# Softmax in whole-tile operations and a pair of tiles half an iteration later, in a four-layer graph network

## What is computed

```python
def _gcn_layer(x, adj, W, b):                      # layer 2: three of them, relu after the first two
    return einsum('bnm,bmh->bnh', adj, x @ W) + b
x = layernorm(x + gcn3(x))
# layer 3: 8 heads of 64
q, k, v = x @ W_qkv
attn = softmax(where(mask, q @ k.T / 8, -big)) * 0.33
attn = attn + 0.33 * adj + 0.33 * exp(-adj)        # both masked
x = layernorm(x + (attn @ v) @ W_out + b_out)
```

## Time and profile before

| | us |
|---|---|
| median of three executions | 2944.71 |
| the profiled execution | 2944.47 |
| its span | 2942.7 |
| TensorE busy | 2735.9 (93% of the span) |
| VectorE busy | 1913.0 (65%) |
| ScalarE busy | 865.3 (29%) |
| GpSimd busy | 729.1 (25%) |

### The profile page before, as it was taken

One profiled execution on the slowest core, in us unless ns is written; L12 is line 12 of the kernel. 1 busy time (PEld: TensorE's weight loads), 2 busy tenths in 40 slices (PEclk: granted clock), 3 DMA queues, 4 the chain that ended last, 5 costly groups with the idle time before them and its releaser, 6 DMA issues.

```text
span 2942.7 us, 74056 instructions
## 1 busy us (share of the span) xinstructions
PE 2735.9 (93%) x30424; PEld 2283.0 (78%) x30424; DVE 1913.0 (65%) x4010; ACT 865.3 (29%) x2429; POOL 729.1 (25%) x1069
## 2 busy tenths in 40 slices
PE   6999999999999999579999999999999999999998
PEld 4778788778888778467877887887787788788777
DVE  5888888888888888545545545554554554554465
ACT  2222222222222222223323323332332332333233
POOL 1222222333333333122122213212211220321221
PEclk9999999999999999889999999999999999999999
DMA  5000000001000000111001001101100100110100
GB/s 172 27 30 30 30 31 32 31 30 30 31 30 31 30 31 30 50 50 36 12 26 37 27 11 37 32 10 33 37 19 19 37 30 8 37 32 10 33 30 16
DMA packets 102612, 95.21 MB, mean 32 GB/s; under 512 B 61712, under 2 KB 63760, under 8 KB 102416
## 3 DMA queue, kind: packets, MB, share of 16 engines
q1 hardware_dynamic: 102416, 92.10, 10.2%
HBM read 58.48 MB, written 33.55 MB: 31 GB/s over the span
## 4 chain that ended last, share of the span: by engine, by line
PE 46%; DVE 6%; issue 3%; ACT 2%; SPq 1%; POOL 1%; DMA 0%; DVEq 0%; POOLq 0%
PE qs L1115 38%; PE qs L1146 4%; ACT E L980 2%; PE qs L1177 1%; PE qs L1156 1%; DVE Z L1095 1%; DVE sm L1021 1%; PE qs L1184 1%; DVE E L1075 1%; DVE Z L1090 1%; PE qs L1191 1%; DVE E L1079 0%; DVE E L1064 0%; DVE sm L1066 0%; ACT H L960 0%
## 5 line engine op out<-in xcount | busy, mean ns | idle before, releaser
L1115 PE MATMUL qs<-hi,T2h 128*128 128x512 f32 x1024 | 431.3, 421 | 14.2 <-DVE T2l L1018 14.2
L1115 PE MATMUL qs<-lo,T2h 128*128 128x512 f32 x1024 | 414.8, 405 | 0.0
L1115 PE MATMUL qs<-hi,T2l 128*128 128x512 f32 x1024 | 413.1, 403 | 0.0
L1018 DVE TENSOR_TENSOR T2l<-qs,T2h 128x512 fp32r<-128x512 f32 x320 | 212.3, 684 | 228.9 <-ACT T2h L956 135.9
L869 POOL TENSOR_SCALAR sm<-sm 128x1 f32<-128x1 f32 x128 | 29.9, 234 | 1282.7 <-DVE sm L1023 1282.7
L1115 PE MATMUL qs<-T2h,WQh 128*128 128x256 f32 x1024 | 292.8, 286 | 0.0
L1115 PE MATMUL qs<-T2l,WQh 128*128 128x256 f32 x1024 | 289.9, 283 | 0.0
L1115 PE MATMUL qs<-T2h,WQl 128*128 128x256 f32 x1024 | 289.8, 283 | 0.0
L1115 PEld LDWEIGHTS qs<-hi,T2h 128*128 128x128 f32 x1024 | 199.6, 195 | 64.9 <-DVE T2l L1018 16.9
L1115 PEld LDWEIGHTS qs<-hi,T2l 128*128 128x128 f32 x1024 | 199.7, 195 | 47.9
L1115 PEld LDWEIGHTS qs<-lo,T2h 128*128 128x128 f32 x1024 | 200.4, 196 | 40.7
(11 more groups left out here) (182 smaller groups left out, 6006.2 us busy)
## 6 DMA issues: line engine op xcount, KB each, us to landing
X<-in_x SPq DMA_DIRECT2D x64, 256.0 KB, 2.6
x<-R SPq DMA_DIRECT2D x64, 256.0 KB, 2.0
X<-x SPq DMA_DIRECT2D x64, 256.0 KB, 2.7
out<-Z SPq DMA_DIRECT2D x64, 256.0 KB, 2.2
AB<-in_adj SPq DMA_DIRECT2D x256, 8.0 KB, 1.5
A<-in_adj SPq DMA_DIRECT2D x128, 32.0 KB, 2.5
A<-in_adj SPq DMA_DIRECT2D x128, 16.0 KB, 1.9
E<-in_L_W1T SPq DMA_DIRECT2D x4, 512.0 KB, 8.0
```

The costliest lines, as they stand in the source:

```text
L1018: return dve.tensor_tensor(lo, ps, hi.bitcast(F32), ALU.subtract)
L1115: mm = pe.matmul(out, lhsT, rhs, start=i == 0, stop=i == len(terms) - 1)
```

## The change

Three things, all in the second half.

1. Softmax: VectorE subtracts the maxima from all heads in one operation (instead of making negative biases), ScalarE takes one exponential over the whole tile (512 columns) instead of eight of 64 columns with a sum each, VectorE sums in one reduction, multiplies by the reciprocals, and the last sum with the adjacency part also multiplies by 0.33.
2. The normalisations x3 and x4: `tensor_scalar` with two per-row scalars becomes `scalar_tensor_tensor` whose second tensor is the reciprocal root, broadcast over the 512 columns.
3. A new `ORDER`. The softmaxes of a pass no longer stand together: those of tiles 0 and 1 come at its beginning, those of tiles 2 and 3 in its middle. qk.0 moves to the end of the pass, as an entry of the next iteration. So that both pairs can hold queries and keys at once, the pair 0 keeps its in the unused heads of `E`, and `AA` is used by pair and tile.

```diff
         ORDER = order(
-            "t2.1 x3.0 b3.3 t1.3 g1.2 xp.0 rs3.1 g1.3 g2.1 z3.1 t2.2 t2.3 v.0 x3.1 xp.1 rs3.2 g2.2 bo.0 rs3.3 z3.2 v.1 x3.2 "
-            "g2.3 xp.2 z3.3 rs4.0 x3.3 qk.0 xp.3 v.2 v.3 s.0 bo.1 s.1 sm.0 bo.2 sm.1 qk.1 ta.0 rs4.1 ta.1 s.2 av.0 av.1 bo.3 "
-            "s.3 wo.0 wo.1 sm.2 z4.0 sm.3 ta.2 x4.0 cm.0+ ta.3 rs4.2 at.0+ av.2 z4.1 t0.0+ av.3 x4.1 wo.2 z4.2 g0.0+ rs4.3 "
-            "t0.1+ wo.3 b3.0+ t1.0+ z4.3 x4.2 t0.2+ b3.1+ x4.3 g0.1+ b3.2+ g1.0+ rs3.0+ t1.1+ t0.3+ g0.2+ g0.3+ t1.2+ t2.0+ "
-            "g1.1+ g2.0+ z3.0+")
+            "s.0 t1.3 sm.0 g1.2 g1.3 ta.0 t2.2 t2.3 av.0 s.1 g2.2 z3.2 g2.3 sm.1 z3.3 rs3.2 wo.0 x3.2 rs3.3 ta.1 x3.3 xp.2 "
+            "bo.2 av.1 xp.3 z4.0 v.2 rs4.0 x4.0 bo.3 v.3 wo.1 z4.1 at.0+ rs4.1 x4.1 qk.1 t0.0+ s.2 t0.1+ b3.0+ sm.2 b3.1+ "
+            "g0.0+ g0.1+ ta.2 t1.0+ t1.1+ av.2 s.3 sm.3 g1.0+ wo.2 z4.2 g1.1+ ta.3 rs4.2 t2.0+ t2.1+ x4.2 av.3 t0.2+ g2.0+ "
+            "wo.3 z3.0+ rs3.0+ g2.1+ z4.3 x3.0+ rs4.3 z3.1+ xp.0+ b3.2+ x4.3 rs3.1+ bo.0+ x3.1+ g0.2+ t0.3+ b3.3+ xp.1+ v.0+ "
+            "bo.1+ v.1+ g0.3+ qk.0+ cm.0+ t1.2+")
...
+        def qk_rows(p, m, n=1):
+
+            if p == 0:
+                return QK[:, m:m + n, :]
+            return E[:, m // 2, HEADS // 2:HEADS, :].rearrange("p (m r) j -> p m (r j)", m=2)[:, m % 2:m % 2 + n, :]
...
-                        for h in range(HEADS):
-                            last = act.activation(EH(c)[:, h, :], EH(c)[:, h, :], ACT.Exp, bias=col(c, NB + h), scale=SCALE,
-                                                  accum_out=col(c, SUM + h))
-                        last.then_inc(ex_ok, 1)
+                        act.activation(EH(c), EH(c), ACT.Exp, scale=SCALE).then_inc(ex_ok, 1)
...
-                        dve.tensor_scalar(X[:, c, :], X[:, c, :], col(c, MV), col(c, RS), ALU.subtract, ALU.mult).then_inc(x3_ok, 1)
+                        dve.scalar_tensor_tensor(X[:, c, :], X[:, c, :], col(c, MV), col(c, RS).to_broadcast([P, D]), ALU.subtract, ALU.mult).then_inc(x3_ok, 1)
...
-                        dve.tensor_scalar(col(c, NB, HEADS), col(c, NMX, HEADS), -SCALE, None, ALU.mult).then_inc(nb_ok, 1)
+                        dve.tensor_tensor(EH(c), EH(c), col(c, NMX, HEADS).unsqueeze(2).to_broadcast([P, HEADS, C]), ALU.subtract).then_inc(nb_ok, 1)
...
                         dve.wait_ge(ex_ok, n[c])
+                        dve.tensor_reduce(col(c, SUM, HEADS), EH(c), AX.X, ALU.add).then_inc(sum_ok, 1)
+                        dve.wait_ge(sum_ok, n[c])
                         dve.reciprocal(col(c, REC, HEADS), col(c, SUM, HEADS)).then_inc(rec_ok, 1)
                         dve.wait_ge(rec_ok, n[c])
-                        dve.tensor_scalar(col(c, RLA, HEADS), col(c, REC, HEADS), LA, None, ALU.mult).then_inc(rla_ok, 1)
...
-                        dve.tensor_tensor(E4(c), E4(c), over_heads(Cm, c), ALU.add).then_inc(attn_ok, 1)
+                        dve.scalar_tensor_tensor(E[:, c, 0:HEADS // 2, :], E[:, c, 0:HEADS // 2, :], LA, over_pairs(Cm, c), ALU.mult, ALU.add)\
+                            .then_inc(attn_ok, 1)
```

More of the change, by code:

```diff
@@ L730, in convolutions_and_attention @@
         MC, VE, RS = range(3)
-        MV, BN, NMX, NB, SUM, REC, RLA = 4, 8, 16, 24, 32, 40, 48
+        MV, BN, NMX, SUM, REC = 4, 8, 16, 24, 32
         def col(c, k, n=1):
@@ L929, in AV @@
         def AV(c):
-            return AA[:, c % 2, 0:HEADS // 2, :].rearrange("p h r -> p (h r)")
+            return AA[:, c // 2, c % 2 * 4:c % 2 * 4 + 4, :].rearrange("p h r -> p (h r)")
+        def qk_rows(p, m, n=1):
+            if p == 0:
+                return QK[:, m:m + n, :]
+            return E[:, m // 2, HEADS // 2:HEADS, :].rearrange("p (m r) j -> p m (r j)", m=2)[:, m % 2:m % 2 + n, :]
         def scores(c):
@@ L937, in over_heads, with over_pairs @@
             return W[:, c, :, :].rearrange("p g j -> p (g j)").unsqueeze(1).unsqueeze(1).to_broadcast([P, 2, 2, P])
+        def over_pairs(W, c):
+            return W[:, c, :, :].rearrange("p g j -> p (g j)").unsqueeze(1).to_broadcast([P, HEADS // 2, P])
         def by_pair(ps):
@@ L975, in steps @@
                             act.wait_ge(qk_ps[b], pair[ahead][c])
-                            act.copy(QK[:, 2 * b:2 * b + 2, :], by_pair(bank(c, b))).then_inc(qk_sb[b], 1)
+                            act.copy(qk_rows(c, 2 * b, 2), by_pair(bank(c, b))).then_inc(qk_sb[b], 1)
                     if step == "sm":
                         act.wait_ge(nb_ok, n[c])
-                        for h in range(HEADS):
-                            last = act.activation(EH(c)[:, h, :], EH(c)[:, h, :], ACT.Exp, bias=col(c, NB + h), scale=SCALE,
-                                                  accum_out=col(c, SUM + h))
-                        last.then_inc(ex_ok, 1)
+                        act.activation(EH(c), EH(c), ACT.Exp, scale=SCALE).then_inc(ex_ok, 1)
                     if step == "ta":
@@ L1059, in steps @@
                             dve.wait_ge(qk_ps[b], pair[ahead][c])
-                            dve.tensor_copy(QK[:, 2 * b:2 * b + 2, :], by_pair(bank(c, b))).then_inc(qk_sb[b], 1)
+                            dve.tensor_copy(qk_rows(c, 2 * b, 2), by_pair(bank(c, b))).then_inc(qk_sb[b], 1)
                     if step == "s":
@@ L1094, in steps @@
                         dve.wait_ge(rs4, n[c])
-                        dve.tensor_scalar(Z[:, c % 2, :], Z[:, c % 2, :], col(c, MV), col(c, RS), ALU.subtract, ALU.mult)\
+                        dve.scalar_tensor_tensor(Z[:, c % 2, :], Z[:, c % 2, :], col(c, MV), col(c, RS).to_broadcast([P, D]), ALU.subtract, ALU.mult)\
                             .then_inc(x4_ok, 1)
@@ L1177, in steps @@
                             mm = pe.matmul(ps[c][y * C:(y + 1) * C, x, (n_ * 2 + g) * C:(n_ * 2 + g + 1) * C],
-                                           QK[x * C:(x + 1) * C, m, rows_g], QK[x * C:(x + 1) * C, KD + m, rows_g], start=True, stop=True)
+                                           qk_rows(c // 2, m)[x * C:(x + 1) * C, 0, rows_g], qk_rows(c // 2, KD + m)[x * C:(x + 1) * C, 0, rows_g], start=True, stop=True)
                         mm.then_inc(s_ps, 1)
@@ L1192, in steps @@
                                            H[rows_g, c, h * DHEAD:(h + 1) * DHEAD],
-                                           AA[rows_g, c % 2, x * 2 + n_, y * C:(y + 1) * C], start=True, stop=True)
+                                           AV(c)[rows_g, (x * 2 + n_) * P + y * C:(x * 2 + n_) * P + (y + 1) * C], start=True, stop=True)
                         mm.then_inc(av_ps, 1)
```

8 lines of the change are left out of this document (3 added, 5 removed).

## The result

The changed kernel takes 3007.17 us (median of four executions, 3005.16 to 3014.43) where the kernel before took 2942.04 beside it (2936.16 to 2948.69): a ratio of 1.0225, 95% interval 1.0196 to 1.0254. The forecast was 2967 and its range ended at 2995, so the direction was right and the size wrong by 40 us. The profiled execution took 3007.52 us, its span is 3005.7.

What follows compares the result with a forecast made beforehand. The prediction took the second half as bound by TensorE, so only PE's idle and slow stretches count. Branch +26, waits -18 and START and END +14 made +22 on 2944.47: 2967 us, own range 2949 to 2985, stated range 2926 to 2995.

Steps and rivals of the forecast that it cites:

- The branch: Loop's taken branch, now behind short matmuls: 6.5 us for 4.6, +1.9 a branch, x14 = +26 us.
- the second idle time: PE's wait for the next code block, 1.85 us behind 23 matmuls after the branch; taken as 0 in the new order.
- The slow clock behind the branch: TensorE's matmuls after the branch's idle time: 2.1 us lost a branch, bounds 1.0 and 3.5.
- Rivals 2 and 3: At the branch: the first, it stays hidden, 2915 us, chance 0.06; the second, block's end falls early again, 2993, chance 0.12.
- The waits: PE's waits in the loop apart from the branch: 3.0 us a pass for 4.2, -1.2 x15 = -18 us.
- xp.2, av.1, xp.3 and v.2 lose 0.9: PE steps delayed 0.9 us a pass because x3.2 and x3.3 stand on VectorE behind z3.3's statistics.
- lands 2.6 later, 1.2 before t0.2: Tile 2's load of X on SyncE's queue: lands 2.6 us after z4.2 is summed, 1.2 before t0.2 needs it.
- The relu waits and s.2: In each pass t2.3, t1.1 and t2.1 wait 0.55 us each for a relu; s.2 waits 0.5 for qk.1's last copy.
- START and END: The stretches before and after the loop: 52.7 and 72.8 us for 29.4 and 81.8, together +14 (9 to 20).
- Softmax: VectorE +1.1 us and ScalarE -2.05 a tile, chain 6.2 for 7.2; counts only through waits of PE, ta's hidden.
- Normalisations: x3 and x4 on VectorE: 0.75 us each for means of 0.81 and 1.15, VectorE -1.8 us a pass.
- Rival 4: VectorE comes late, behind its list by the longer softmax: waits of 5.0 us a pass, +30, 2997 us, chance 0.08.

Runs made afterwards that it cites:

- e6: The kernel before with 100 waits (51 instructions by the trace) that wait for nothing on TensorE ahead of the loop: 2958.9 us, ratio 1.0028.
- e9: The kernel before with 300 waits (151 instructions by the count) that wait for nothing on TensorE ahead of the loop: 2890.95 us, ratio 0.9804.
- e7: The changed kernel with GpSimd's bo.2 and bo.0 moved so that neither runs beside a normalisation of X: 2976.6 us, ratio 1.0088.
- e3: The kernel before with only the whole-tile softmax, its order and buffers kept: 3003.28 us, ratio 1.0204.
- e5: The changed kernel with the old softmax and old normalisations, so the new order and its buffers alone: 3035.59 us, ratio 1.0322.
- e2: The changed kernel with x3 and x4 back as tensor_scalar: 2990.11 us, ratio 1.0165.
- e4: The kernel before with only x3 and x4 as scalar_tensor_tensor: 2965.36 us, ratio 1.0051.
- The repaired new order: The changed kernel with qk.0 and t1.2 heading the pass, bo.2 and bo.0 moved off X's normalisations, x3 and x4 as tensor_scalar: 2888.17 us, ratio 0.9794.
- e11: The repaired new order with t0.2 of the next tiles also put behind g2.0: 2885.55 us, ratio 0.9788.

## Why the prediction was wrong, by its steps

**The branch: right in its mechanism, and nearly in its size.** Idle time in front of s.0 was forecast at 4.4 and is 4.39. "I take 0" for the second idle time, with the block end 210 instructions on, held; e6 and e9 bear out that reading of the block on the kernel before. The slow clock behind the branch was forecast at 2.1 and costs 1.5. Both together are 6.0 for 6.5, some 7 us less in 14 passes. Rivals 2 and 3 are excluded by the trace.

**The waits: the step that failed.** The forecast was 3.0 us a pass for 4.2, so a pass of 99.0 without a branch. The one such pass is 100.8, and in 15 passes that is 27 us, the larger part of the miss. The failed sentence is "x4 takes 1.15 and x3 0.81 on average; as scalar_tensor_tensor 0.75 each". In the kernel before the two forms of time stand side by side (ns min/median/max):

```profile
L1053 DVE TENSOR_SCALAR X<-X,sm x64: 535/545/1509, 1296.4 to 2889.1; 128x512 f32<-128x512 f32 x64
L1095 DVE TENSOR_SCALAR Z<-Z,sm x64: 511/1174/1515, 1359.5 to 2939.7; 128x512 f32<-128x512 f32 x64
```

So the mean of 0.81 already mixed 0.54 with 1.5, and 0.752 for L416 came from an operation that ran nearly always undisturbed (median 0.746). I had read the mean as the form's own price and not asked what ran beside it. So "xp.2, av.1, xp.3 and v.2 lose 0.9" became 2.5 with xp.1, +1.6 a pass or 24 us, and v.2's slow clock in six passes made 8 more. e7 shows the size: moving two sums of GpSimd takes some 31 us away, to 2976.6, which is inside the forecast's own range.

"lands 2.6 later, 1.2 before t0.2" failed too: t0.2 waits 0.74 a pass, 11 us. The relu waits and s.2 came out smaller than the floor put them (1.35 for 1.65, 0.25 for 0.5). The remaining 0.8 a pass of the 1.8 is, as far as the list of waits shows, a difference of counting: the forecast's 3.0 was from start to start, the list of waits takes ends that are modelled some 0.1 late, and there are eight waits a pass.

**START and END** were 54.8 and 73.5 for 52.7 and 72.8: 3 us more than forecast.

**Softmax.** The chain's length did not matter and ta's cover held in the new order, as forecast ("hidden at nothing"). That it counts "only through waits of PE" held as well. What the text did not see is that its sign hangs on the order: +62 us in the old (e3), -45 in the new (e5 against e2).

**Normalisations: the wrong sign.** They cost 15 us in the old order (e4) and 17 in the new (e2), not nothing. The sentence that spoke against them in the prediction, the higher rate of the two-scalar form from the Trainium skill ("VectorE: DVE Perf Modes", the perf-mode tier table), agrees in its direction with the rows that have nothing large beside them: 0.51 to 0.55 us for 0.72 to 0.75, which is less than twice the rate.

Rival 4 (VectorE late, waits of 5.0 a pass, 2997) was nearest in the place of the waits and in their sum (4.8), yet not in the cause: the wait for X is 23.2 us with the old softmax (e5) and 23.3 with the new (e2), and e7 takes it away by moving GpSimd's sums alone. In sum, +27 for the pass without a branch, +11 for the load of X, +8 for v.2's clock, +2 for relu waits that are 0.16 longer behind a branch, -7 for the branch, +3 for the ends and -2 in the untouched first half make 42; the miss is 40.

## What to carry to other kernels

- **Cut a hardware loop where TensorE's long matmuls end.** The sequencer leads by a number of instructions (14 to 16 matmuls here), and what that hides is their time: 3.3 us of 512 columns, 0.3 us of 64. Then look where a block of code ends behind the head. The same loop gives a ratio of 1.0028, 1 or 0.9804 with 51, 0 or 151 inert instructions in front of it, so a change of any kind can be credited with up to 2% that belong to its place.
- **A mean is not a price.** Look at minimum, median and maximum of a VectorE form and at what GpSimd does at that time before costing another form by it; then move GpSimd's large sums away, which was worth 31 us here for one edit of a list.
- **Compare like with like before pricing a branch.** The first pass has no taken branch, but here it also lacked a wait for a load and a slow stretch that ten and six of the later passes have, together 1.4 of the 7.4 us.
- **Ask a moved order for its ends too.** The repaired new order has passes of 99.8 us for the 101.0 of e9, 18 us in 15 passes, and START and END of 127.8 for 110.2. In 16 iterations the one pays for the other.

## What the runs showed of the chip

- A taken branch of the second half's loop, with 2248 recorded instructions of TensorE a pass, takes 3.3 to 4.0 us of its sequencer; the first half's, with 1618, takes 0.21. With a block end some 54 instructions behind the head (a count from the trace and the block's estimated size) there comes a second idle time of 1.85; with it 3 behind, one of 3.4 to 4.4 in one piece; with it some 150 behind, none. "Runtime: NRT & Kernel Launch" of the Trainium skill (Instruction fetch mechanics) speaks of a fetch at such a branch; that the next block is waited for separately is what e6 and e9 add.
- Behind one idle time of 1.07 us the granted clock stayed at 2.4 GHz (e9). Behind 0.99 and 1.85 with 23 small matmuls between them, and behind 4.4 alone, it was 1.2 GHz for some 3 us, behind some branches for over 5. Behind the 1.34 of xp.3, with 0.30 and 36 small matmuls before it, it fell in six passes of fifteen and stayed in nine.
- VectorE's tensor_scalar and scalar_tensor_tensor over 128x512 take 0.51 to 0.55 and 0.72 to 0.75 us with no large GpSimd operation beside them, and up to 1.6 and 1.87 beside a GpSimd tensor_tensor over 128x512. That one takes 1.26 to 1.30 mostly, and up to 1.74 in the changed kernel, so both sides can lose.
- Left open: why v.2 meets the lower clock in some passes and not in others, and how the loads of X and the stores of Z share the queue, which was not tried beyond e11.
